# Normalising the softmax rows on ScalarE instead of GpSimd in a fused convolution and attention kernel

## The reference, cut to what matters

```python
# layer 0: 32 small models, 16 channels each, hidden width 64
perception = concat(x shifted by the 9 offsets of a 3x3 window)      # 144 inputs per model
x1 = x + w2 @ relu(w1 @ perception + b1) + b2
# layer 1: attention over the 1024 pixels of an image
theta, phi, g = theta_w @ x1 + theta_b, phi_w @ x1 + phi_b, g_w @ x1 + g_b    # 128 channels each
attn = softmax(theta^T phi, over the last axis)                       # 1024 x 1024
y = attn @ g
z = w_w @ y + w_b ;  z = (z - bn_mean) * bn_gamma / sqrt(bn_var + 1e-5) + bn_beta
out = z + x1
```

## Time and profile before

| | us |
|---|---|
| median of 3 runs | 1478.81 (1477.78 to 1479.68) |
| the profiled execution | 1478.04 |
| its span | 1476.2 |
| TensorE busy | 1431.6 (97%) |
| VectorE busy | 850.8 (58%) |
| ScalarE busy | 743.4 (50%) |
| GpSimd busy | 255.9 (17%) |

### The profile page before, as it was taken

One profiled execution on the slowest core, in us unless ns is written; L12 is line 12 of the kernel. 1 busy time (PEld: TensorE's weight loads), 2 busy tenths in 40 slices (PEclk: granted clock), 3 DMA queues, 4 the chain that ended last, 5 costly groups with the idle time before them and its releaser, 6 DMA issues.

```text
span 1476.2 us, 27078 instructions
## 1 busy us (share of the span) xinstructions
PE 1431.6 (97%) x10364; PEld 792.8 (54%) x10364; DVE 850.8 (58%) x1033; ACT 743.4 (50%) x1175; POOL 255.9 (17%) x134
## 2 busy tenths in 40 slices
PE   7999999999999999999999999999999999999997
PEld 2454646446474564745546465464654647456476
DVE  1374665755656555565646657466574665756555
ACT  3464464644545454455553646446454454555444
POOL 0030220202112031120302203022030211202112
PEclk9999999999999999999999999999999999999999
DMA  4144543436335354344444534454353633536401
GB/s 135 63 146 141 202 147 120 172 116 233 135 114 185 116 205 143 139 168 140 165 143 168 176 125 143 143 200 149 121 172 115 232 129 108 185 119 216 143 29 58
DMA packets 129803, 216.31 MB, mean 147 GB/s; under 512 B 7328, under 2 KB 79008, under 8 KB 129696
## 3 DMA queue, kind: packets, MB, share of 16 engines
q1 hardware_dynamic: 129696, 214.62, 41.9%
HBM read 110.25 MB, written 104.33 MB: 145 GB/s over the span
## 4 chain that ended last, share of the span: by engine, by line
PE 80%; ACT 8%; DVE 7%; issue 4%; DMA 0%; ACTq 0%; SPq 0%
PE ps L444 24%; PE ps L473 7%; PE ps L492 6%; PE ps L493 6%; PE ps L494 6%; PE ps L460 6%; DVE x_lo L899 4%; PE ps L523 4%; PE ps L525 4%; PE ps L524 4%; ACT hidden L693 3%; ACT probs L722 3%; PE ps L511 2%; PE ps L536 2%; DVE g_lo L905 2%
## 5 line engine op out<-in xcount | busy, mean ns | idle before, releaser
L444 PE MATMUL ps<-windows,w_main 64*64 64x512 f32 x4096 | 458.2, 594 | 8.2 <-DMA windows<-in_x 8.2
L1089 POOL TENSOR_TENSOR probs<-probs,row_inv 128x1024 f32<-128x1024 f32 x128 | 255.2, 1999 | 1202.7 <-DVE row_inv L885 1202.7
L693 ACT ACTIVATE hidden<-ps,columns 128x512 f32<-128x512 f32 x512 | 303.3, 702 | 294.9 <-PE ps L460 294.9
L444 PEld LDWEIGHTS ps<-windows,w_main 64*64 64x64 f32 x4096 | 150.6, 132 | 304.7 <-issue 302.8
L879 DVE TENSOR_REDUCE neg_max<-ps 128x1 f32<-128x1024 f32 x128 | 155.3, 1218 | 134.1 <-PE ps L513 131.8
L722 ACT ACTIVATE probs<-ps,neg_max 128x1024 f32<-128x1024 f32 x128 | 144.0, 1145 | 147.3 <-DVE neg_max L879 147.3
L890 DVE STREAM_TRANSPOSE probs<-probs 128x1024 f32<-128x1024 f32 x120 | 144.9, 1225 | 51.3 <-POOL probs L1089 51.3
L899 DVE TENSOR_TENSOR x_lo<-x_lo,x_hi 128x1024 fp32r<-128x1024 f32 x120 | 166.3, 1426 | 0.0
L861 DVE SCALAR_TENSOR_TENSOR x1s<-ps,columns,windows 128x512 f32<-128x512 f32 x128 | 95.4, 745 | 111.4 <-PE ps L473 109.8
L492 PE MATMUL ps<-x_hi,wp_hi 128*128 128x512 f32 x384 | 151.3, 394 | 6.9 <-issue 6.9
L729 ACT CAST x_hi<-x_lo 128x1024 fp32r<-128x1024 f32 x120 | 122.4, 1104 | 63.5 <-DMA x_lo<-rows_out 63.5
(11 more groups left out here) (78 smaller groups left out, 1405.5 us busy)
## 6 DMA issues: line engine op xcount, KB each, us to landing
rows_out<-probs SPq DMA_DIRECT2D x120, 512.0 KB, 3.1
x_lo<-rows_out SPq DMA_DIRECT2D x120, 512.0 KB, 6.1
out<-x1s SPq DMA_DIRECT2D x30, 1024.0 KB, 4.6
windows<-in_x SPq DMA_DIRECT2D x64, 298.0 KB, 4.9
windows<-in_x SPq DMA_DIRECT2D x64, 264.0 KB, 5.7
rows_out<-g_t SPq DMA_DIRECT2D x15, 512.0 KB, 3.1
g_raw<-rows_out SPq DMA_DIRECT2D x15, 512.0 KB, 5.4
out<-x1s SPq DMA_DIRECT2D x8, 256.0 KB, 2.2
```

The source lines that it names most:

```text
L444: product = mm(ps[HIDDEN * which:HIDDEN * (which + 1), hidden_bank(n, s, q), :], w_main[rows, p, which, :], shifted(windows[rows, chunk % ...
L693: activation(hidden[:, s % HIDDEN_HELD, q, :], ps[:, hidden_bank(n, s, q), :], ACT.Relu, bias=b1s[:, column:column + 1]).then_inc(hidden_r ...
L1089: nc.gpsimd.tensor_tensor(rows, rows, row_inv[:, e].to_broadcast([P, PIXELS]), ALU.mult).then_inc(normalized, 1)
```

## The change

`normalize` is taken from GpSimd's queue to ScalarE's. It is no longer a product with a broadcast tensor, but an activation `Copy` with the inverse as its scale, one value per partition. The waits and the semaphore that it raises are the same. GpSimd's loop is gone. ScalarE's queue gets 8 more instructions per image, and the written orders of all queues are set anew around them; TensorE's order is changed in the last image alone.

```diff
 # SyncE, each image
                 send_row(n, 0)
+                send_g(n)
                 send_row(n, 1)
-                send_g(n)
                 fetch_row(n, 0)
                 send_row(n, 2)
                 send_row(n, 3)
+                fetch_row(n, 1)
                 fetch_g(n)
-                fetch_row(n, 1)
...
                 send_row(n, 5)
+                send_row(n, 6)
                 fetch_row(n, 4)
-                send_row(n, 6)
                 send_row(n, 7)
 # TensorE, last image
             project(LAST, 1, TH)
+            project(LAST, 1, G)
             scores(LAST, 2)
-            project(LAST, 1, G)
             turn_row(0)
+            turn_g()
             scores(LAST, 3)
-            turn_g()
             turn_row(1)
             scores(LAST, 4)
+            scores(LAST, 5)
             turn_row(2)
-            scores(LAST, 5)
+            attend_turned(0)
             turn_row(3)
             scores(LAST, 6)
-            attend_turned(0)
             turn_row(4)
             scores(LAST, 7)
+            turn_row(5)
             attend_turned(1)
-            turn_row(5)
+            turn_row(6)
             last_outputs(0)
-            turn_row(6)
+            turn_row(7)
             attend_turned(2)
-            turn_row(7)
             attend_turned(3)
 # ScalarE
+            def normalize(n, i):
+                act.wait_ge(inv_done, n * QBLOCKS + i + 1)
+                rows, e = probs[:, i % ROWS_HELD, :], slice(i % ROWS_HELD, i % ROWS_HELD + 1)
+                activation(rows, rows, ACT.Copy, scale=row_inv[:, e]).then_inc(normalized, 1)
 # ScalarE, each image
                 exp_row(n, 0)
-                exp_row(n, 1)
+                normalize(n, 0)
                 bias_projection(n, 0, G)
                 bias_projection(n, 1, TH)
+                exp_row(n, 1)
                 exp_row(n, 2)
                 bias_projection(n, 1, G)
+                normalize(n, 1)
                 exp_row(n, 3)
+                normalize(n, 2)
+                normalize(n, 3)
                 relus(n + 1, 0)
...
                 exp_row(n, 7)
+                normalize(n, 4)
                 round_g(n)
                 round_row(n, 1)
                 round_row(n, 2)
                 round_row(n, 3)
                 relus(n + 1, 2)
+                normalize(n, 5)
+                normalize(n, 6)
                 relus(n + 1, 3)
+                normalize(n, 7)
                 round_y(n, 0)
 # ScalarE, last image
             bias_projection(LAST, 1, PH)
+            exp_row(LAST, 0)
             bias_projection(LAST, 0, G)
-            exp_row(LAST, 0)
             bias_projection(LAST, 1, TH)
             exp_row(LAST, 1)
+            normalize(LAST, 0)
+            bias_projection(LAST, 1, G)
+            normalize(LAST, 1)
+            round_turned_row(0)
             exp_row(LAST, 2)
...
 # VectorE, each image
                 invert_sum(n, 0)
+                find_max(n, 2)
                 invert_sum(n, 1)
-                find_max(n, 2)
                 transpose_row(n, 0)
+                invert_sum(n, 2)
                 split_projection(n, 1, TH)
-                invert_sum(n, 2)
-                transpose_row(n, 1)
                 transpose_g(n)
                 find_max(n, 3)
+                transpose_row(n, 1)
...
                 find_max(n, 7)
+                invert_sum(n, 5)
                 sum_x1(n + 1, 1 - parity, 0)
+                sum_x1(n + 1, 1 - parity, 1)
                 split_row(n, 0)
-                invert_sum(n, 5)
-                sum_x1(n + 1, 1 - parity, 1)
                 split_g(n)
...
                 transpose_row(n, 4)
+                invert_sum(n, 7)
                 transpose_row(n, 5)
                 transpose_row(n, 6)
+                transpose_row(n, 7)
                 sum_x1(n + 1, 1 - parity, 2)
+                split_y(n, 0)
                 sum_x1(n + 1, 1 - parity, 3)
-                invert_sum(n, 7)
-                split_y(n, 0)
-                transpose_row(n, 7)
...
                 split_x1(n + 1, 1 - parity, 2)
+                sum_x1(n + 1, 1 - parity, 6)
                 split_x1(n + 1, 1 - parity, 3)
                 add_out(n, parity, 1, 0)
-                sum_x1(n + 1, 1 - parity, 6)
                 add_out(n, parity, 1, 1)
 # GpSimd
-            def normalize(n, i):
-                pool.wait_ge(inv_done, n * QBLOCKS + i + 1)
-                rows, e = probs[:, i % ROWS_HELD, :], slice(i % ROWS_HELD, i % ROWS_HELD + 1)
-                nc.gpsimd.tensor_tensor(rows, rows, row_inv[:, e].to_broadcast([P, PIXELS]),
-                                        ALU.mult).then_inc(normalized, 1)
...
-            with pool.Fori(0, BATCH) as n:
-                for i in range(QBLOCKS):
-                    normalize(n, i)
```

More of the change, by code:

```diff
@@ L825, in _ @@
             bias_projection(LAST, 1, PH)
+            exp_row(LAST, 0)
             bias_projection(LAST, 0, G)
-            exp_row(LAST, 0)
             bias_projection(LAST, 1, TH)
             exp_row(LAST, 1)
+            normalize(LAST, 0)
+            bias_projection(LAST, 1, G)
+            normalize(LAST, 1)
+            round_turned_row(0)
             exp_row(LAST, 2)
-            bias_projection(LAST, 1, G)
-            round_turned_row(0)
+            round_turned_g()
             round_turned_row(1)
-            round_turned_g()
             exp_row(LAST, 3)
+            normalize(LAST, 2)
+            exp_row(LAST, 4)
             round_turned_row(2)
-            exp_row(LAST, 4)
+            normalize(LAST, 3)
+            exp_row(LAST, 5)
             round_turned_row(3)
-            exp_row(LAST, 5)
+            normalize(LAST, 4)
+            normalize(LAST, 5)
+            round_turned_y(0)
             round_turned_row(4)
-            round_turned_y(0)
             exp_row(LAST, 6)
+            normalize(LAST, 6)
+            round_turned_row(5)
             exp_row(LAST, 7)
             round_turned_y(1)
-            round_turned_row(5)
             round_turned_row(6)
+            normalize(LAST, 7)
             round_turned_row(7)
@@ L950, in batch @@
                 invert_sum(n, 0)
+                find_max(n, 2)
                 invert_sum(n, 1)
-                find_max(n, 2)
                 transpose_row(n, 0)
+                invert_sum(n, 2)
                 split_projection(n, 1, TH)
-                invert_sum(n, 2)
-                transpose_row(n, 1)
                 transpose_g(n)
                 find_max(n, 3)
+                transpose_row(n, 1)
+                invert_sum(n, 3)
                 transpose_row(n, 2)
-                invert_sum(n, 3)
                 transpose_row(n, 3)
@@ L976, in batch @@
                 transpose_row(n, 4)
+                invert_sum(n, 7)
                 transpose_row(n, 5)
                 transpose_row(n, 6)
+                transpose_row(n, 7)
                 sum_x1(n + 1, 1 - parity, 2)
+                split_y(n, 0)
                 sum_x1(n + 1, 1 - parity, 3)
-                invert_sum(n, 7)
-                split_y(n, 0)
-                transpose_row(n, 7)
                 add_out(n, parity, 0, 0)
+                add_out(n, parity, 0, 1)
                 split_row(n, 4)
+                add_out(n, parity, 0, 2)
                 sum_x1(n + 1, 1 - parity, 4)
-                add_out(n, parity, 0, 1)
-                add_out(n, parity, 0, 2)
+                add_out(n, parity, 0, 3)
                 sum_x1(n + 1, 1 - parity, 5)
-                add_out(n, parity, 0, 3)
                 split_row(n, 5)
@@ L1051, in _ @@
             invert_sum(LAST, 0)
-            find_max(LAST, 2)
             split_projection(LAST, 1, TH)
             invert_sum(LAST, 1)
-            invert_sum(LAST, 2)
+            find_max(LAST, 2)
             split_turned_row(0)
             find_max(LAST, 3)
+            invert_sum(LAST, 2)
+            split_turned_g()
             split_turned_row(1)
+            find_max(LAST, 4)
+            find_max(LAST, 5)
             invert_sum(LAST, 3)
-            find_max(LAST, 4)
             split_turned_row(2)
-            split_turned_g()
             invert_sum(LAST, 4)
-            find_max(LAST, 5)
+            invert_sum(LAST, 5)
+            split_turned_row(3)
             find_max(LAST, 6)
-            split_turned_row(3)
-            invert_sum(LAST, 5)
+            split_turned_y(0)
+            split_turned_row(4)
+            invert_sum(LAST, 6)
             find_max(LAST, 7)
-            split_turned_row(4)
-            split_turned_y(0)
-            invert_sum(LAST, 6)
+            split_turned_row(5)
             split_turned_y(1)
             invert_sum(LAST, 7)
-            split_turned_row(5)
+            split_turned_row(6)
             for k in range(BLOCKS):
                 add_last_out(0, k)
-            split_turned_row(6)
             split_turned_row(7)
```

## The result

| | before | after |
|---|---|---|
| median, us | 1478.98 | 1464.89 (1463.96 to 1465.51) |
| ratio, 95% interval | 1 | 0.9905 [0.9888, 0.9922] |
| span of the profiled execution | 1476.2 | 1462.1 |

A forecast was written before the change was run, and what follows sets the result against it. TensorE, busy 1431.6 of 1476.2 us, was taken as the bound, so only its idle time could move. Steady images -10.5 and the last image -2.5 gave -13.0, hence 1465.8 us; range 1462.5 to 1472.5.

The forecast's parts named there:

- The stall before attend: TensorE's 0.70 us wait before the first product of `attend(n, 0)` in 15 images, 10.5 in all, laid to GpSimd's queue.
- ScalarE's price 1.02: Assumed cost in us of one 128x1024 `Copy` normalisation on ScalarE, with ends 0.94 and 2.00.
- Cover at attend 0.9: Slack before attend: VectorE's chain of splits was to end at 738.76, against TensorE ready at 739.67.
- Cover at `dx` of step 3 0.75: Slack between the end of step 3's relus, behind normalisations of rows 5 and 6, and the `dx` needing them.
- Table loads: Rival: `Copy` in another ScalarE table than the exponential, 15 us of loads per image, above 1510; chance 0.01.
- End of the image 0: `sum_x1` ahead of the last `split_x1`, cover 0.13 before TensorE's next projection: loss taken as 0, ends 0 and +0.2 per image.
- The last image -2.5: New lists in the last image bring the last attend to 1463.8 instead of 1466.34.
- upper end of its range, +1: Worst end for the last image's term: each of six normalisations half a microsecond dearer.
- Sum: Steady images -10.5 and last image -2.5, together -13.0 us.
- Cost 0: Verdict on the normalisations of rows 0 to 3, and on SyncE's sends and fetches: no time lost.
- GpSimd's part goes: With no GpSimd instruction in the loop, four VectorE splits before attend take 4.9 instead of 7.38, -2.5 on that chain.
- The slower rival: Splits before attend stay slow for a cause other than GpSimd, +12.8, 1492 us; chance 0.08.

The follow-up runs named there:

- e2: Kernel before, old orders, with GpSimd's normalisation cut to 8 of 1024 columns in the first 15 images: 1466.5 us, 0.9912.
- e3: Changed kernel plus a GpSimd product on its own 128x1024 tile after each inverse in the first 15 images: 1475.84 us, 0.9975.
- e6: Changed kernel plus two idle ScalarE copies between the normalisation of row 4 and g's rounding, first 15 images: 1480.04 us, 1.0006.
- e7: Changed kernel plus one idle ScalarE copy between the normalisation of row 6 and the relus of step 3, first 15 images: 1472.02 us, 0.9953.
- e1: All new orders of the changed kernel, but GpSimd normalises as in the kernel before: 1465.45 us, 0.9907.
- e13: Kernel before with row 5's reciprocal directly behind the last maximum and `sum_x1` of group 1 ahead of row 0's split: 1468.8 us, 0.9935.
- e11: Changed kernel with VectorE's and SyncE's orders in the first 15 images as in the kernel before: 1489.15 us, 1.0072.
- e12: Kernel before with one VectorE line moved, row 5's reciprocal directly behind the last maximum: 1479.38 us, 1.0003.
- e4: Changed kernel plus a one-column GpSimd product, then two write-only 128x1024 memsets, after each inverse in the first 15 images: 1464.46 us, 0.9899.
- e8: Changed kernel with TensorE's order mains 0, left 0, mains 1, left 1 in the first 15 images: 1459.31 us, 0.9866.
- e10: The kernel of e8 with TensorE's loop over pairs of images written out in full: 1454.14 us, 0.9833.

## Why the prediction was right, point by point

- *The stall before attend is GpSimd's.* Right, shown by e2 (without it, no stall) and e3 (foreign work brings it back, 0.72 of idle time per image). Its size is right too: 0.70 was forecast, 0.71 came from image to image.
- *ScalarE's price 1.02.* Measured 1.04. *Cover at attend 0.9*: 0.92 by e6. It holds by two errors that nearly cancel: the four splits took 4.68 and not 4.9, and the hand-over of 0.14 was left out. *Cover at `dx` of step 3 0.75*: 0.58 by e7.
- *Table loads.* None came with `Copy`: ScalarE's only two, at L817 and L818, stand ahead of the loop, as they did before the change.
- *End of the image 0.* TensorE's next projection starts at 774.69 with no gap; the fourth split of x1 ends at 774.47.
- *The last image -2.5.* -2.57; the last attend starts 30.0 us after the first turn, 29.9 was worked out. The turns between, walked through the lists by hand, are right to 0.2: 3.4, 8.2, 11.9, 15.3, 18.8, 22.6 and 26.2 after the first, where the forecast had 3.4, 8.1, 11.8, 15.3, 18.7, 22.5 and 26.1. Only the upper end of its range, +1, is looser than its own working: six times half a microsecond on -2.5 is +0.5.
- *Sum.* -13.0 against -14.1. Of the 1.1, about 0.2 is 15 x 0.01 and the 0.07 of the last image; the rest is the 0.8 of L492 and the program's start, which the prediction has no term for and which I can't tell from chance.
- *What was wrong: the reading of the change.* The prediction counted the moved VectorE lines at nothing, by "Cost 0" or by their cover, and laid the whole steady gain on "GpSimd's part goes". e1 and e13 show a second cause among those lines that is nearly enough by itself (0.66 of the 0.77): the reciprocal of row 5 ahead of both `sum_x1` takes GpSimd out of g's split. With it, GpSimd could have stayed (e1: 1465.45 against 1464.89, not told apart by the clock; 0.08 per image by the traces). And e11 shows that without the moved lines of VectorE and SyncE the move to ScalarE makes the kernel 10 us slower, not 14 faster; the prediction had no term for what stands behind the transpose of row 1. That this did not show in the number is luck: either cause alone removes most or all of the same stall, which can only be removed once.
- *The slower rival* (the splits stay slow, 1492) did not come. e3 shows what its case would have cost: with other reads on GpSimd the changed kernel's row splits are slow and the chain is late by 0.7. The time is 1475.84 and not 1492, as the reordered reciprocal keeps g's split short.

## What to carry to other kernels

When two engines take turns, the cheapest cure may be to move the short instruction that starts the other engine, so that its work falls beside work that doesn't collide; count where each overlap goes next, since e12 moved it and gained nothing. When a change moves an instruction and reorders the queues, test each part alone before giving either the credit: two causes that each give most of one gain look like one. And an instruction that comes later on a busy engine than it did on an idle one makes its consumers late, and all that stands behind them in their queues: that must be moved past them too (e11).

## What the runs showed of the hardware

- A GpSimd product that reads 128x1024 from SBUF and a VectorE difference of two SBUF tiles take turns: 5.17 us for three differences with one product among them (before, e1, e3), 3.48 with memsets beside them (e4). It didn't matter whose tile was read (e3).
- A wait can cost TensorE more than the idle time before its first product: 0.65 for 0.28 between two `dx` (e7), but 0.71 for 0.70 ahead of attend.
- TensorE's product starts 0.14 to 0.15 us after the end of the VectorE instruction that it waits for (before, e1, e6, e13).
- A one-column product on GpSimd took 1.01 us beside VectorE's differences and 0.19 without (e4).
- VectorE's transposes, maxima and `sum_x1` (one SBUF operand at most) kept their 1.2, 1.2 and 0.74 us with GpSimd beside them (e1).
- Two more changes between products of 64 and of 32 rows cost TensorE 0.34 us (e8); an end of its loop about 0.6 (3.6 over six, e8 against e10).
